# Moving the loads of x from SyncE's DMA queue to ScalarE's, and the second one to the weights

## The reference, cut to what matters

```python
xn = layernorm(x)                                   # per token
q, k, v = xn @ Wq, xn @ Wk, xn @ Wv                 # 16 heads of 16
attn = softmax(q . k over the last 64 positions)    # sliding window, causal
ctx  = (attn @ v) @ Wo
h    = layernorm(gelu(xn @ ternary(W_fc).T)) * ln_w + ln_b
out  = x + ctx + h @ ternary(W_proj).T
```

## Time and profile before

| what | value |
|---|---|
| median of three runs | 439.74 us |
| the profiled execution: its time, its span | 440.41 us, 438.6 us |
| mean granted TensorE clock | 0.984 |
| TensorE matmul busy | 387.7 us (88%) |
| VectorE busy | 348.8 us (80%) |
| ScalarE busy | 327.2 us (75%) |
| GpSimd busy | 182.5 us (42%) |
| issues of x_in | 8, 512 KB each, median 9.3 us from issue to landing |
| issues of k_stack and q_stack | 96, 128 KB each, 7.5 and 4.7 us |

### The profile page before, as it was taken

The page is one execution under the profiler, slowest core; times in us unless marked ns, Lnnn a source line. Parts: engine busy times, 40 slices in busy tenths (PEclk is TensorE's granted clock), DMA queues, the critical chain, the costliest instruction groups (busy, mean ns, idle before and its releaser), DMA issues.

```text
span 438.6 us, 13237 instructions
## 1 busy us (share of the span) xinstructions
PE 387.7 (88%) x5692; PEld 266.4 (61%) x5692; DVE 348.8 (80%) x679; ACT 327.2 (75%) x407; POOL 182.5 (42%) x110
## 2 busy tenths in 40 slices
PE   0389699799999999899989999899989998898885
PEld 0236256466656677467656677567755766666674
DVE  7977687597887799589968899689958997669864
ACT  2234179868896788778897789778896889779861
POOL 2700003546163262437154344427244716335851
PEclk9999799999998999999999999999999999999999
DMA  7119207900392009700591029400880049001002
GB/s 272 63 42 121 67 3 99 141 3 1 67 120 57 14 29 129 124 13 17 91 150 24 13 58 128 95 13 28 119 133 16 1 92 120 22 13 50 16 31 67
DMA packets 30682, 29.19 MB, mean 67 GB/s; under 512 B 5664, under 2 KB 29280, under 8 KB 30624
## 3 DMA queue, kind: packets, MB, share of 16 engines
q1 hardware_dynamic: 30624, 28.35, 39.0%
HBM read 7.35 MB, written 4.19 MB: 26 GB/s over the span
## 4 chain that ended last, share of the span: by engine, by line
PE 37%; DVE 21%; SPq 17%; DMA 16%; issue 5%; ACT 3%; POOL 1%; POOLq 0%; DVEq 0%; ACTq 0%
SPq L330 12%; DMA x_in<-in_x 10%; PE small L1049 9%; PE big L989 7%; DMA k_stack<-qk_split 6%; DVE negmax L691 5%; PE big L963 3%; PE small L1060 3%; SPq L345 3%; PE big L1008 3%; PE big L1002 3%; DVE y_bufs L730 3%; PE small L1076 2%; DVE g_lo L685 2%; DVE ctxn L741 2%
## 5 line engine op out<-in xcount | busy, mean ns | idle before, releaser
L429 POOL TENSOR_TENSOR p_parts<-probs,p_parts 128x1024 f16<-128x1024 f32 x64 | 137.1, 2154 | 93.3 <-ACT p_parts L539 93.3
L538 ACT ACTIVATE probs<-big,exp_scale 128x1024 f32<-128x1024 f32 x64 | 71.5, 1117 | 29.9 <-PE big L1032 29.8
L691 DVE TENSOR_REDUCE negmax<-big 128x8 f32<-128x1024 f32 x64 | 77.1, 1221 | 7.6 <-PE big L1008 6.7
L539 ACT ACTIVATE p_parts<-big,exp_scale 128x1024 f16<-128x1024 f32 x64 | 71.5, 1117 | 0.0
L1049 PE MATMUL small<-proj_t,g_hi 128*128 128x256 f16 x256 | 59.2, 278 | 0.2 <-DVE ctxn L741 0.2
L1049 PE MATMUL small<-proj_t,g_lo 128*128 128x256 f16 x256 | 58.8, 276 | 0.0
L989 PE MATMUL big<-fc_t,xt_hi 128*128 128x512 f16 x128 | 49.8, 389 | 3.0 <-DVE negmax L691 2.8
L989 PE MATMUL big<-fc_t,xt_lo 128*128 128x512 f16 x128 | 49.5, 387 | 0.0
L516 ACT ACTIVATE gel<-big 128x1024 f32<-128x1024 f32 x32 | 32.7, 1024 | 20.9 <-PE big L989 20.2
L685 DVE SCALAR_TENSOR_TENSOR g_lo<-big,lnw_s,g_hi 128x512 f16<-128x512 f32 x64 | 44.9, 742 | 0.1
L553 ACT ACTIVATE g_hi<-big,lnw_s 128x512 f16<-128x512 f32 x64 | 39.6, 690 | 2.4 <-PE big L1039 2.3
(11 more groups left out here) (130 smaller groups left out, 833.5 us busy)
## 6 DMA issues: line engine op xcount, KB each, us to landing
q_stack<-qk_split SPq DMA_DIRECT2D x48, 128.0 KB, 4.7
k_stack<-qk_split SPq DMA_DIRECT2D x48, 128.0 KB, 7.5
x_in<-in_x SPq DMA_DIRECT2D x8, 512.0 KB, 9.3
out<-y_bufs SPq DMA_DIRECT2D x32, 128.0 KB, 1.8
v_odd<-v_even SPq DMA_DIRECT2D x16, 132.0 KB, 4.8
v_odd<-v_even SPq DMA_DIRECT2D x16, 99.0 KB, 4.7
gel<-in_w_fc SPq DMA_DIRECT2D x1, 1024.0 KB, 7.1
y_bufs<-in_w_proj SPq DMA_DIRECT2D x1, 1024.0 KB, 8.9
```

The costliest lines, as they stand in the source:

```text
L429: g.tensor_tensor(p_lo[:, j % PB], probs[:, j % PB], p_hi[:, j % PB], ALU.subtract).then_inc(*sig(p_lo_ready))
L538: s.activation(probs[:, j % PB].rearrange("p i (u q) -> p u i q", u=2), st, ACT.Exp, scale=exp_scale[:, 0:1]).then_inc(*sig(exp_ready))
L539: s.activation(p_hi[:, j % PB].rearrange("p i (u q) -> p u i q", u=2), st, ACT.Exp, scale=exp_scale[:, 0:1]).then_inc(*sig(p_hi_ready))
L691: v.tensor_reduce(negmax[:, :, j], slot[b, "sa", j][:].rearrange("p a (u k) -> p (a u) k", k=P), AX.X, ALU.max, negate=True).then_inc(*sig ...
```

## The change

x of batch 1 is issued by SyncE behind the second feed-forward weight and ahead of the copies of the masks. x of batches 2 to 7 is no longer issued by SyncE at all: ScalarE's own DMA queue issues it, with the same two waits, after the second pair of exponentials of batch b-2. The rest of SyncE's order stays.

```diff
         @block.sync
         def _(sp):
-            @per_batch
-            def load_x(b):
-                if b >= 2:
-                    wait(sp, b - 2, xn_ready, 1)
-                    wait(sp, b - 2, res_ready, 1)
-                sp.dma_start(x_in[:, b % 2], x[b].rearrange("(t p) d -> p t d", p=P)).then_inc(*sig(x_loaded[b % 2]))
-
-            @per_batch
-            def load_next_x(b):
-                load_x(b + 1)
+            def load_first_x(b):
+                sp.dma_start(x_in[:, b], x[b].rearrange("(t p) d -> p t d", p=P)).then_inc(*sig(x_loaded[b]))
...
-            load_x(0)
+            load_first_x(0)
             load_weights(0)
             load_ffn(0)
             load_weights(1)
             load_norm()
             load_ffn(1)
+            load_first_x(1)
             copy_masks()
...
                 load_stack(p - 1, 1, 1)
-                load_next_x(p - 1)
                 shift_values(p - 1, 0)
...
         @block.scalar
         def _(act):
             s = nc.scalar
+
+            @per_batch
+            def load_x(b):
+                wait(act, b - 2, xn_ready, 1)
+                wait(act, b - 2, res_ready, 1)
+                act.dma_start(x_in[:, b % 2], x[b].rearrange("(t p) d -> p t d", p=P)).then_inc(*sig(x_loaded[b % 2]))
...
                 exp(p, 1)
+                load_x(p + 2)
                 exp(p, 2)
```

## The result

The changed kernel takes 449.58 us (median of four runs, 446.92 to 451.55) against 440.27 us of the kernel before on the same chip: a ratio of 1.0195, 95% interval 1.0158 to 1.0232. It is slower by some 9 us. The forecast was 438.9 us, "no change that can be told", with a range up to 447.0, so the time lies outside; it is close to the 448.2 us of the rival "turn by turn in the engines", though, as the runs show, for another reason. (Ratios here leave out disturbed runs, of which the profiled one of the first "SyncE, ahead of all stacks" is one, and medians keep them, so the two can differ by up to 0.7%.)

What follows compares the result with a forecast made beforehand. TensorE's fixed order, with its wait for the stacks, was taken as the bound. The terms -2.8 - 1.1 - 1.8 + 3.6 + 1.3 gave -0.8, from 440.41 to 439.6 us, forecast as 438.9 against the median; range 433.5 to 447.

Steps and rivals of the forecast that it cites:

- turn by turn in the engines: Rival, at the wait ahead of `sa` 0: engines alternate queues, x goes wholly ahead of the last stack; 448.2 us, chance 0.15.
- What bounds the kernel: In each period TensorE's fixed order sets the time; VectorE's 30.1 us of waiting for x hardly reaches it.
- x of batch 1, -2.8: In the prologue, x issued with the weights removes TensorE's 2.8 us wait at `fc` piece 2.
- The clock behind it, -1.1: After the prologue's standstill, the clock's fall up to 55.5 us may stay away: -1.1 us, bounds 0 and 2.2.
- When x starts: On ScalarE's queue, x of batches 2 to 7 starts between 221.2 and 223.7 us, against 223.16 before.
- When it lands: In the period shown, x on its own queue should land between 228 and 230.5 us, against 231.50 before.
- The queue of its own changes nothing: Rival, batches 2 to 7: x comes out behind the stacks as before, only the prologue gains; 435.8 us, chance 0.06.
- What the stacks pay, +3.6: Ahead of `sa` 0, x in flight delays the last stack 0.6 us in six periods, a third of 1.7: +3.6 us.
- What it gives, -1.8: In the periods, x landing earlier removes TensorE's three waits at `st` 4 for VectorE's maximum: -1.8 us.
- ScalarE pays 0: One 0.54 us issue per period on ScalarE is covered by its idle time before the fourth pair: 0 us.
- Falls of the clock, +1.3: With later stacks TensorE stands still longer; one more period has a clock fall: +1.3 us, bounds 0 and 5.2.
- ScalarE is held up: Rival, ScalarE's issue: it waits, so the fourth pair comes about 1 us late each period; 444.9 us, chance 0.04.

Runs made afterwards that it cites:

- SyncE, ahead of all stacks: Kernel before with x of batch 1 beside the weights, x of batches 3 to 7 on SyncE's queue before all stack transfers: 435.17 us, repeated 434.00.
- one pair earlier: Changed kernel with ScalarE's issue of x behind the first pair of exponentials instead of the second: 454.73 us, ratio 1.0208.
- later x left out: Kernel before with x of batch 1 issued with the weights and x of batches 2 to 7 not loaded at all: 437.11 us, ratio 0.9860.
- x 1 alone: Kernel before with only x of batch 1 moved to the weights, x of batches 2 to 7 on SyncE's queue as before: 437.30 us, ratio 0.9900.
- ahead of all stacks, ScalarE's queue: Changed kernel with ScalarE's issue of x of batches 3 to 7 moved before the stack transfers, batch 2 still behind the second pair: 438.65 us, ratio 0.9911.
- ScalarE's queue alone: Changed kernel with x of batch 1 put back where it was, x of batches 2 to 7 on ScalarE's queue: 458.49 us, ratio 1.0382.
- one pair later: Changed kernel with ScalarE's issue of x behind the third pair of exponentials instead of the second: 446.72 us, ratio 1.0152.
- behind the first gelu: Changed kernel with ScalarE's issue of x moved behind the next batch's first gelu: 445.04 us, ratio 1.0061.

## Why the prediction was wrong, point by point

*What bounds the kernel.* Right. TensorE's order sets the periods, the wait for the stacks is its largest, VectorE's wait for x hardly counts. Two runs show it: one pair earlier, 24 us of VectorE's waiting are gone and the kernel is no faster than the changed one; with later x left out, the 25.1 us of x 1 alone are gone, and the medians are 437.11 and 437.30.

*x of batch 1, -2.8.* Right; alone it gave 437.30 us, 3.6 us under the 440.94 of the kernel before in that call.

*The clock behind it, -1.1.* In the changed kernel 0: it fell again, to 0.50 from 48 to 53 us. With x of batch 1 alone it did not. Both are inside the bounds that were given; the middle between them was a guess.

*When x starts.* Right, 225.12 us, just before the second pair. *When it lands, "between 228 and 230.5".* **This is the step that failed.** It took for granted that with a queue of its own x no longer stands behind the stacks. It does: no packet of x moved for 5.2 us, and 9.65 us passed from issue to statistics, against 8.3 before; VectorE's wait for x stayed at 24.4 us, where under 8 was forecast. The prediction named this possibility ("The queue of its own changes nothing", 0.06) but for one side only, x behind the stacks. It missed that an order set by issue, between two engines, is a race that goes either way, and that ScalarE's issue, which it placed "not before 221.2" against SyncE's x at 223.16, would come while SyncE still had stacks to issue.

*What the stacks pay, +3.6.* Measured +8.3, mostly in four periods, at 1.8 to 2.2 us each: the full price of 1.7, or a little more, or nearly nothing, never the third that was taken as a mean. This is the term of the sum in which that step shows. The argument from the two rates (120 and 321 GB/s) asked how two transfers in flight together share the engines. All but a small part of them was not in flight together. The Trainium skill (DMA: Bandwidth & Descriptors, "Queues, rings and completion order") says that each DMA engine goes round the queues that it has work for, by packet. Had x been work for them from its issue on, it would have been under way within its next microseconds beside the stacks. The trace shows nothing of that: 566 packets of SyncE's queue and none of ScalarE's from 225.5 to 230.0 us. The Trainium skill (DMA: Bandwidth & Descriptors, "Issuing engines are not separate DMA queues") says that a second issuing engine saves nothing but time of issue. The runs agree: ahead of all stacks, ScalarE's queue gives 438.65 us, SyncE's 434.00.

*What it gives, -1.8.* -1.1: one of three waits stayed, in the last of the two periods in which x came behind the stacks.

*ScalarE pays 0.* Right: its issue took 0.41 us in 225.12 to 225.53, beside a running instruction, and the engine's 327.0 us of work are the 327.2 of before.

*Falls of the clock, +1.3.* Too small. Counted by TensorE's busy time they are 6.2 us, above the upper bound of 5.2; together with the -1.1 above, the sum had +0.2 for the clock. The reading that longer waits bring more of them was right in direction, but their number is not in the stacks' wait alone: the half with ScalarE's queue alone has the same 20.7 us and 8.7 us more of busy time.

*The sum.* It said -0.8 and the two profiled executions differ by +10.1. Of that miss of 10.9 us the stacks make 4.7, `st` 4 0.7 and the clock 6.0 (0.5 too many, as the account above does not close to the tenth). So the clock is the largest part by number. It goes with the wait for the stacks: the four kernels with over 20 us of that wait had a mean clock of 0.941 to 0.969 in all their executions, those with under 14 us 0.962 to 0.992. How much of the one comes from the other no run shows.

*The rival "turn by turn".* Its place and its time (448.2 against 449.58) came out, its mechanism did not, and the time is in part luck: it had 1.5 us in each of six periods (9.0, measured 8.3, nearly all from four), falls of 5.2 (measured 6.2), and a gain of 5.7 in the other parts (measured 3.9).

What stays open: why SyncE and ScalarE have one common order. The runs show that they nearly do, not where it is made (in generating the descriptors, or in the engines). And when exactly the clock falls: two kernels with the same 20.7 us of waiting for the stacks differ by 8.7 us in TensorE's busy time, and two executions of one and the same kernel, with 13.3 and 13.6 us of that waiting, by 5.0 us (391.7 and 386.7), at 440.08 and 435.25 us. So differences of a few us in that column are no property of a kernel, and no run was made that moves the clock alone.

## What to carry to other kernels

A transfer that is moved to another engine's DMA queue does not get past a backlog: look at what is issued before it, on every queue, and at who waits for the transfers that it gets ahead of. If two queues issue at about the same time, the order is a race, and each period can fall on another side; place the issue where the other queue has nothing to send. And before paying for an earlier landing, ask whether the engine that waits for it is the one that sets the time: here some 25 us of its waiting cost TensorE 1.8 us.

## What was not expected

Where an issue of SyncE takes long, the order follows its end, not its start. SyncE's last two k_stack issues take 2.69 us from 224.33 and so end at 227.02; ScalarE's x begins and ends within the second of them, at 225.12 and 225.53, and lands first (three more pairs in the other runs are like it):

```profile
224.33 2.69 SPq L322 DMA_DIRECT2D k_stack<-qk_split  x2
```

The order is not strict where two issues are close. Their landings came against the ends of the issues in five pairs that ended within 0.1 us of each other, and then some 80 to 140 KB of the other queue moved in the midst of x, so "wholly ahead or wholly behind" does not hold there. In four pairs a stack whose issue ended 0.4 to 1.3 us behind that of x landed before it, by up to 1.6 us, though the bulk of x had gone ahead: x's last few packets trail. In the run one pair earlier, from 225 to 229 us, behind the burst:

```profile
q1 hardware_dynamic: 475, 0.43, 111.7%
q10 hardware_dynamic: 21, 0.02, 4.8%
```

An issue can hold its engine for long. In the run one pair later, ScalarE's first one took 8.03 us, and the engine, which had the rest of its third pair in hand, then stood still for 4.28:

```profile
75.05 8.03 ACTq L482 DMA_DIRECT2D x_in<-in_x  x1
...
77.74 1.15 ACT L537 ACTIVATE p_parts<-big,exp_scale 128x1024 f16<-128x1024 f32 x1
83.17 1.28 ACT L514 ACT_TABLE_LOAD   x1 [4.28 <-issue]
```

TensorE waited 1.3 us for the gelu behind it. In the run behind the first gelu the first issue took 4.80 us. All others of these two runs on ScalarE took about 0.4 us. The rival "ScalarE is held up" exists, then, but it was not what made the changed kernel slow, where that first issue took 0.43 us. SyncE shows the like for x of batch 1 in the changed kernel, where one issue took 4.41 us behind the weights; there nothing waited for it.
